# Projecting V eight key tiles at a time and only in some steps of a two-layer cross attention

## What is computed

```python
def _lora_linear(x, W, A, B):
    return x @ W + SCALING * (x @ A @ B)
# layer 0
q = _lora_linear(hidden_states, Wq, Aq, Bq); k, v = the same of the context with 8 heads
attn = softmax(q k^T / 4); out = hidden_states + _lora_linear(attn v, Wo, Ao, Bo)
# layer 1, on the output of layer 0, the same context
Q, K, V = x @ Wq.T + bq, ctx @ Wk.T + bk, ctx @ Wv.T + bv
scores = where(mask, Q K^T / 4, -inf)
y = x + softmax(scores) V @ Wo.T + bo
return (y - mean(y)) / sqrt(var(y) + 1e-5) * ln_g + ln_b
```

## Time and profile before

| | |
|---|---|
| Time, median of 3 runs | 1937.78 us (1935.24 to 1938.48) |
| The profiled execution: its time, and its span | 1935.51 us, 1933.7 us |
| TensorE busy | 1825.2 us, 94% of the span |
| VectorE busy | 1268.2 us, 66% |
| ScalarE busy | 1027.6 us, 53% |
| GpSimd busy | 186.0 us, 10% |
| TensorE clock granted | 0.973 of full speed on average |

### The profile page before, as it was taken

The page is one execution under the profiler, slowest core; times in us unless marked ns, Lnnn a source line. Parts: engine busy times, 40 slices in busy tenths (PEclk is TensorE's granted clock), DMA queues, the critical chain, the costliest instruction groups (busy, mean ns, idle before and its releaser), DMA issues.

```text
span 1933.7 us, 43919 instructions
## 1 busy us (share of the span) xinstructions
PE 1825.2 (94%) x18340; PEld 1134.5 (59%) x18340; DVE 1268.2 (66%) x2743; ACT 1027.6 (53%) x2040; POOL 186.0 (10%) x268
## 2 busy tenths in 40 slices
PE   6899999999999999999999999999999999999985
PEld 3556455565454655555566666666667566666652
DVE  1566666666677777766665667767676767767751
ACT  0055555555555555555554555655555555655562
POOL 2010111102120001021100100001000100001001
PEclk8799999999999999999999999999999999999996
DMA  6911325212352222225422544233533236324300
GB/s 189 243 46 27 78 61 156 52 23 65 78 149 37 42 44 61 42 77 145 84 48 47 107 75 88 41 54 50 110 54 54 38 54 121 48 34 64 50 6 11
DMA packets 65030, 138.13 MB, mean 71 GB/s; under 512 B 12540, under 2 KB 49436, under 8 KB 64832
## 3 DMA queue, kind: packets, MB, share of 16 engines
q1 hardware_dynamic: 64832, 135.33, 34.5%
HBM read 97.84 MB, written 34.89 MB: 69 GB/s over the span
## 4 chain that ended last, share of the span: by engine, by line
PE 84%; ACT 6%; DVE 5%; issue 2%; DMA 2%; SPq 1%; POOL 1%; POOLq 0%
PE value L733 21%; PE work L644 12%; PE score L710 11%; PE work L627 11%; PE score L715 10%; PE ring L690 7%; ACT p_sb L799 4%; PE work L666 3%; PE work L764 3%; DVE chunk_max L904 3%; PE ring L678 2%; PE ring L743 1%; PE work L650 1%; DMA ctx_sb<-ctxT 1%; DMA k_stack<-k_dram 1%
## 5 line engine op out<-in xcount | busy, mean ns | idle before, releaser
L799 ACT ACTIVATE p_sb<-score 124x512 f32<-124x512 f32 (+1 forms) x1664 | 905.3, 597 | 746.6 <-PE score L710 391.0
L904 DVE TENSOR_REDUCE chunk_max<-ring 128x1 f32<-128x402 f32 x2048 | 1071.3, 571 | 318.1 <-PE ring L690 296.2
L690 PE MATMUL ring<-k_stack,q_stack 64*128 64x402 f32 x2048 | 766.3, 433 | 18.9 <-DVE chunk_max L904 13.5
L733 PE MATMUL value<-p_sb,v_sb 124*32 124x256 f32 x6656 | 447.4, 390 | 0.0
L690 PEld LDWEIGHTS ring<-k_stack,q_stack 64*128 64x128 f32 x2048 | 349.1, 186 | 64.9 <-DVE chunk_max L904 52.2
L715 PE MATMUL score<-q_stack,k_stack 64*124 64x256 f32 (+1 forms) x1664 | 332.2, 316 | 19.0 <-ACT p_sb L799 16.4
L710 PE MATMUL score<-q_stack,k_stack 64*124 64x512 f32 (+1 forms) x832 | 331.0, 466 | 9.9 <-ACT p_sb L799 7.9
L644 PE MATMUL work<-wv,ctx_sb 64*124 64x128 f32 x3840 | 323.2, 281 | 9.4 <-ACT v_sb L828 1.7
L644 PEld LDWEIGHTS work<-wv,ctx_sb 64*124 64x124 f32 x3840 | 284.0, 185 | 37.9 <-PE work L644 17.8
L715 PEld LDWEIGHTS score<-q_stack,k_stack 64*124 64x124 f32 (+1 forms) x1664 | 219.3, 184 | 138.7 <-ACT p_sb L799 71.6
L627 PE MATMUL work<-ctx_sb,wk 64*128 64x402 f32 x1280 | 284.9, 515 | 15.7 <-DMA ctx_sb<-ctxT 9.3
(11 more groups left out here) (68 smaller groups left out, 598.8 us busy)
## 6 DMA issues: line engine op xcount, KB each, us to landing
k_stack<-k_dram SPq DMA_DIRECT2D x288, 200.1 KB
k_dram<-k_parts SPq DMA_DIRECT2D x60, 402.0 KB, 3.0
ctx_sb<-ctxT SPq DMA_DIRECT2D x24, 992.0 KB, 6.2
k_dram<-k_parts SPq DMA_DIRECT2D x20, 395.0 KB, 2.6
q_stack<-few_rows SPq DMA_DIRECT2D x256, 2.0 KB
wq<-l_Wq SPq DMA_DIRECT2D x2, 1024.0 KB, 10.0
xt_sb<-xT SPq DMA_DIRECT2D x4, 512.0 KB, 12.3
wo<-l_Wo SPq DMA_DIRECT2D x2, 1024.0 KB, 7.0
```

The costliest lines, as they stand in the source:

```text
L690: engine.matmul(ring[bank_of["max", n]][:, 0:MW], q_stack[rows, u % 3, j, q * P:(q + 1) * P], k_stack[rows, 2 * (z % 3) + (u % 2 if u < L0 ...
L733: done = engine.matmul(value_bank[32 * j:32 * j + 32, 0:S], v_sb[0:tn, seq % 2, i, head * VW:head * VW + 32], p_sb[0:tn, (2 * n + j % 2) % ...
L799: engine.activation(p_sb[0:tn, n % PLACES, :], score_bank[n % 2][0:tn, :], ACT.Exp, scale=SCALE).then_inc(s_exp, 1)
L904: engine.tensor_reduce(chunk_max[:, u % 2, half, j * QT + q, c:c + 1], ring[bank_of["max", n]][:, 0:MW], AX.X, ALU.max).then_inc(s_taken[" ...
```

## The change

V of a sequence becomes two products in place of seven (`groups`): the first has eight tiles, four in each bank of `work` with 128 columns each, and 32 pieces; the second has tiles 8 to 11, two in each bank, and the last tile behind them in the second bank, 20 pieces. There is one swap of the halves in each, and the last tile waits for the pieces before it. ScalarE reads each bank with one instruction (the last tile with one more), without a scale by validity; the added column of ones keeps it, and masked keys have the score -1e30 added. The first product spans two chunks of the context and frees both together.

The rate of the background is multiplied by 13/7 in free steps and is zero in value steps. Budget that is left over can still be spent there. A finished product is read at once in the order of steps. In the prologue there is no V product ahead of the first max.

```diff
+        self.groups = []
+        for first in range(0, NT, 2 * CT):
+            n = min(2 * CT, NT - first) // 2
+            single = first + 2 * n if first + 2 * n == NT - 1 and NT - first < 2 * CT else None
+            self.groups.append((first, n, single))
...
-        values = [("v", 0, g) for g in range(-(-self.NT // 2))]
-        self.product(*values[0])
-        self.product(*values[1])
-        ahead = [(name, p) for name in values[2:] for p in range(self.pieces(name))]
+        ahead = [(("v", 0, g), p) for g in range(len(self.groups)) for p in range(self.pieces(("v", 0, g)))]
...
-    COST = {"k": 670, "v": 213, "q": 213, "o": 853}
+    COST = {"k": 670, "v": 218, "q": 218, "o": 853}
...
                 self.current, self.stopped = None, True
+                self.flush()
...
+        free = [i for i in range(NT) if (i - 1) % NT not in self.ends]
...
-                rate, self.stopped = self.plan_rate(), False
+                rate, self.stopped = self.plan_rate() * (NT / len(free) if i in free else 0), False
...
-        def halves(p):
-
-            swap = p // KT
-            return ((swap, HALF[0], p % KT), (1 - swap, HALF[1], p % KT))
+        def halves(p, tiles=1):
+
+            swap, j, k = p // (KT * tiles), p // KT % tiles, p % KT
+            return ((swap, HALF[0], j, k), (1 - swap, HALF[1], j, k))
...
+                    first, tiles, single = plan.groups[g]
+                    if p < 2 * KT * tiles:
+                        swapped(e, ("v", seq, g), p, tiles)
+                        for n, rows, j, k in halves(p, tiles):
+                            t0 = tile(first + n * tiles + j)[0]
+                            done = engine.matmul(work[0:TT, n, j * P:(j + 1) * P], ctx_sb[rows, k, t0:t0 + TT],
+                                                 w[rows, k, col * P:(col + 1) * P], start=(p == 0),
+                                                 stop=(p == 2 * KT * tiles - 1 and (n == 0 or single is None)))
...
+                        if k == 0 and tiles:
+                            e.wait_ge(s_made["v"], made["v", seq, g] - 1)
...
-                    if seq >= B:
-                        b = (seq - B) // 4
-                        e.wait_ge(s_taken["turn mask"], 1)
-                        engine.activation(dst, src, ACT.Copy, scale=valid[0:tn, b, i:i + 1])\
-                            .then_inc(s_taken["v"], 1)
+                    engine.activation(
+                        v_sb[0:tn, seq % 2, i:i + count, 0:8 * VW].rearrange("p i (h e) -> p i h e", e=VW)[:, :, :, 0:HD],
+                        work[0:tn, bank, block * P:(block + count) * P].rearrange("p (i h d) -> p i h d", i=count, d=HD),
+                        ACT.Copy).then_inc(s_taken["v"], 1)
```

More of the change, by code:

```diff
@@ L51, in step, with tiles_of, readings @@
         self.steps.append(name)
-    def banks_of(self, name):
-        return 1 if name[0] == "v" and 2 * name[2] + 1 == self.NT else 2
+    def tiles_of(self, name):
+        return self.groups[name[2]] if name[0] == "v" else (0, 1, None)
+    def readings(self, g):
+        first, n, single = self.groups[g]
+        return ([(0, 0, first, n), (1, 0, first + n, n)] if n else []) + \
+            ([(1, n, single, 1)] if single is not None else [])
     def begin(self, name, banks):
@@ L63, in begin @@
             self.work_owner[n] = name
-        self.count[name[0]] = self.count.get(name[0], 0) + len(banks)
+        ends = len(banks)
+        if name[0] == "v":
+            _, n, single = self.tiles_of(name)
+            ends = 2 * (n > 0) + (single is not None)
+        self.count[name[0]] = self.count.get(name[0], 0) + ends
         self.made[name] = self.count[name[0]]
@@ L77, in read @@
         elif kind == "v":
-            for n in range(self.banks_of(name)):
-                self.step("read v", name[1], 2 * name[2] + n)
+            for n in range(len(self.readings(name[2]))):
+                self.step("read v", name[1], name[2], n)
         elif kind == "q":
@@ L115, in piece @@
                 self.step("ones", name[1])
[L116 to L120, removed]
+            self.begin(name, [0, 1])
+            self.taken[name] = self.made[name] // 2 if name[0] == "q" else self.made[name]
+            if self.tiles_of(name)[1]:
                 self.swap_count += 2
@@ L158, in ctx_of @@
         if kind == "v":
-            return z, [2 * g // self.CT]
+            first, n, single = self.groups[g]
+            return z, sorted({i // self.CT for i in range(first, first + 2 * n + (single is not None))})
         return z, sorted({c for k in (2 * g, 2 * g + 1) for c in self.chunks_of_keys[k]})
     def names_of_ctx(self, z):
-        B, k, v = self.B, range(self.NM // 2), range(-(-self.NT // 2))
+        B, k, v = self.B, range(self.NM // 2), range(len(self.groups))
         if z < B:
@@ L248, in main_products @@
         B, UB, NT, L0, UNITS = self.B, self.UB, self.NT, self.L0, self.UNITS
-        k, v = range(self.NM // 2), range(-(-NT // 2))
+        k, v = range(self.NM // 2), range(len(self.groups))
         todo = self.todo
@@ L624, in tensor @@
                     swapped(e, ("k", seq, g), p)
-                    for n, rows, k in halves(p):
+                    for n, rows, _, k in halves(p):
                         lo = keys_of(2 * g + n)[0]
@@ L635, in tensor @@
                     if p == 0:
-                        z, (c,) = plan.ctx_of(("v", seq, g))
+                        z, chunks = plan.ctx_of(("v", seq, g))
                         bank_free(e, ("v", seq, g))
-                        e.wait_ge(s_ctx[c], 16 * (z + 1))
+                        for c in chunks:
+                            e.wait_ge(s_ctx[c], 16 * (z + 1))
                         weight_ready(e, "v", layer)
[L640 to L647, removed]
-                    else:
-                        t0, tn = tile(2 * g)
-                        done = engine.matmul(work[0:tn, 0, 0:P], ctx_sb[:, p, t0:t0 + tn],
-                                             w[:, p, col * P:(col + 1) * P], start=(p == 0), stop=(p == KT - 1))
-                        if p == KT - 1:
@@ new lines, in tensor @@
+                    first, tiles, single = plan.groups[g]
[6 more added lines that the diff above has]
+                                                 stop=(p == 2 * KT * tiles - 1 and (n == 0 or single is None)))
+                            piece_done(done, "v", p, tiles)
+                    else:
+                        (t0, tn), k = tile(single), p % KT
+                        if k == 0 and tiles:
+                            e.wait_ge(s_made["v"], made["v", seq, g] - 1)
+                        done = engine.matmul(work[0:tn, 1, tiles * P:(tiles + 1) * P], ctx_sb[:, k, t0:t0 + tn],
+                                             w[:, k, col * P:(col + 1) * P], start=(k == 0 and not tiles),
+                                             stop=(k == KT - 1))
+                        if k == KT - 1:
```

29 lines of the change are left out of this document (13 added, 16 removed).

## The result

The changed kernel takes 1943.54 us (median of 20 runs, 1936.52 to 1949.6), the kernel before 1936.05 us in the same measurement (20 runs, 1931.55 to 1942.73). The ratio is 1.0033, with a 95% interval from 1.002 to 1.0046. It is slower by 0.33%, where I forecast 1907 us. The profiled execution's span is 1941.9 us.

What follows compares the result with a forecast made beforehand. TensorE was taken as the bound, except in free steps, set by a score bank's round. Layer 1 -23, layer 0 -9, prologue +5 and V reads -1 gave 1935.5 - 28 = 1907.5, said as 1907 us; range 1872 to 1948.

Steps and rivals of the forecast that it cites:

- Layer 0: Layer 0's units: zero for dense units 3 to 15, -0.5 us each for 16 to 27, -3 for 28 to 35; -9 together.
- The prices of the pieces: TensorE's projection work: 0.214 us for each piece of V, 0.67 us for each K piece.
- The pair's sum: Units 46 and 47 of layer 1: all steps, work, swaps and starts together 52.1 us against 53.4, -1.3 us.
- The starts of V's products: TensorE waiting for ScalarE's reads of both banks when a V product starts: 1.1 us, twice for a pair of units.
- rival (a): Product starts come a step later and their stalls vanish: 36 us less, 1872 us; chance 0.17.
- Layer 1's size: All 26 units counted in layer 1: -0.9 us for each, -23 us, since other units swap more often.
- The prologue: Start of the kernel, V's first two products moved into the loop behind: +5 us, 2 of it for the clock.
- TensorE go cold: Skill rule against the change: without V products over the prologue's wait, the loop starts at half speed, +8 instead of +5.
- The shadow of the fourth max: Value steps with four maxima: hidden places for pieces given up, about 1.3 us a unit; layer 1 still gains at most 0.6.
- Rival (b): Hidden places ahead of the fourth max decide: 81 us of them given up, some 1955 us, slower; chance 0.17.
- The grouping and the free steps: Layer 1: three fewer swaps, 1.05 us a pair; pieces moved into free steps gain at most 0.6 us a unit.

Runs made afterwards that it cites:

- undoing the order in two ways: Changed kernel with finished products read at the end of their step, 1925.03 us; changed kernel with the maxima's transpose and transfer ahead of the projections, 1925.75 us.
- the line alone: The kernel before with one line added, so that a finished product is read at once: 1940.55 us, ratio 1.0032.
- the run with the loads at the end: Changed kernel with product reads and context loads at the end of the step, loads behind the maxima's transfer: 1915.1 us, 0.991 to the kernel before.

## Why the prediction was wrong

**The step that failed** is one that the prediction doesn't have. "A finished product is read at once" stands in the account of the change, and no term of the sum prices it. I followed the read on ScalarE, where it stands behind the scores' exponentials anyway, and didn't follow it past SyncE's queue: the read of a K product issues two writes of K on that queue, which wait for GpSimd (an instruction of 0.9 to 1.0 us after one of 0.5 for each), and behind them, in order, stands the transfer of maxima on which the next unit's first score waits. The same holds for the context's loads, of which three now come in the same step. Shown: undoing the order in two ways gave 16 and 14 us, undoing it for the loads as well gave 24, and the line alone made the kernel before slower by 0.32%.

**Layer 0 without those waits** gained 8.3 us in units 0 to 27 (773.94 to 765.65), 6 were forecast. Units 28 to 35 gained 4.6 in the changed kernel's profile and 1.5 in that of the run with the loads at the end (forecast 3). The prices of the pieces held: 0.214 us forecast, 0.22 measured.

**The pair's sum** came out at 51.92 us against 52.1 (free steps 23.20 and value steps 28.72 us, where its terms make 23.3 and 28.8), but in part by luck. The starts of V's products were priced at 1.1 us, two in a pair, 44 us over 20 sequences. The changed kernel's trace has 6.9 us of TensorE's waits for ScalarE ahead of V's matmuls, in 13 places, and 4.3 us ahead of Q's. Against that stand pieces left in a value step (four in step 4 of unit 47), which the sum had in free steps. So what rival (a) names was there in part, without its 36 us.

**Layer 1's size was wrong.** I carried the pair 46 and 47 (forecast -1.3, measured -1.5 us) to all of layer 1 as -0.9 for each unit. Units 36 to 59 gained 5.8 us, not 22. The twelve units of the pair's kind gained 8.3 us together, 0.7 each; the twelve in whose stretch an output product and a layer norm fall lost 2.5. Nearly all that is missing lies in three of these: units 41, 49 and 57 lost 11.3 us together, and the other 21 of the 24 gained 17.1. In these three VectorE's sums stand ahead of a step with four maxima; moving them gave 4.7 us back there in one pair of profiles and 4.8 in another. The sum had no term for it. What the rest of their loss comes from is open.

**The prologue** was forecast at +5 and cost 0.6 in these profiles. The nine other profiles with the new prologue have the first score at 97.89 to 99.14 us, those of the three others with the old one at 95.75 to 97.25, so 1 to 2 us is nearer. TensorE did wait for the first max up to 61.69 us, as said, 0.8 us less than in the kernel before (62.45). The timeline of TensorE behind it:

```profile
61.69 0.70 PE L713 MATMUL ring<-k_stack,q_stack 64*128 64x402 f32 x2 [9.95 <-issue]
...
63.72 0.71 PE L713 MATMUL ring<-k_stack,q_stack 64*128 64x402 f32 x2
...
65.76 0.71 PE L713 MATMUL ring<-k_stack,q_stack 64*128 64x402 f32 x2
...
67.24 0.44 PE L713 MATMUL ring<-k_stack,q_stack 64*128 64x402 f32 x2
...
68.31 0.48 PE L713 MATMUL ring<-k_stack,q_stack 64*128 64x402 f32 x2
...
74.24 1.14 PE L664 MATMUL work<-wv,ctx_sb 64*124 64x128 f32 x16 [1.03 <-ACT v_sb L844]
```

The turns of the loop take 2.03, 2.04 and 1.48 us and then 1.1 to 1.2, not the 1.24 that I took; two maxima take 1.14. The kernel before had lost time in its own loop, where VectorE was busy for 10.17 of 14.15 us, since swaps and starts of five products stood there. The windows of that loop and of the first two turns in the changed kernel (the columns as above, the granted clock third from the end):

```profile
62.45:76.60 14.15, 12.11 (x157) 9.92 (x158) 10.17 (x20) 2.06 (x9) 0.00 (x0) 1.00 1.05 383
```

```profile
61.69:66.00 4.31, 4.31 (x38) 4.31 (x40) 2.12 (x4) 0.00 (x0) 0.00 (x0) 0.50 1.05 387
```

The slow turns follow 9.95 us in which TensorE stood idle, and cost 0.9 + 0.9 + 0.4 = 2.2 us against turns of 1.1. The clock is at 0.50 in them, its lower level, and at 1.00 in the whole loop of the kernel before. The Trainium skill, "TensorE: Matmul & The Clock Gate", section "Loop structure matters more than you think", has TensorE go cold, to half its clock, over such a wait, and this trace agrees. I had weighed that against the change with 5 us for the loop, and taken 2. The start of the second V product waited 1.03 us for ScalarE (the row at 74.24), where 1.1 was forecast.

**The shadow of the fourth max** was in the forecast as a loss that the others outweigh. That was right in sign: the new wait for VectorE is 32 us. Used together with full free steps it gave 44 us, 0.7 us for each of 62 units. Rival (b) names this mechanism, but it is not why the change lost: with the order mended the kernel gains 17 us without it.

**The grouping and the free steps** were priced as two parts that add up. They don't: alone the groups give -12 us and the free steps +34 us, both together, with reads and loads at the end, -17 us.

**Two sums of the prediction don't come out.** 1907.5 and the 2.3 us of the median make 1909.8, not 1907. Rival (b)'s own terms, +31 - 11.5 + 5 on 1935.5, make 1960, not 1955. Neither touches the account above.

## What to carry to other kernels

A step that moves in a hand-written order moves every instruction that it issues on every engine: go through the list engine by engine, the transfer queue first, and ask what stands behind each one that waits. A place in which nothing is computed may still be a place in which work is hidden: look for the wait in front of the last instruction of a kind (here the fourth max) before all work is taken away from it. And an average over units is a forecast only for units of the same kind; take one window of each kind.

## What the runs showed that I had not expected

SyncE's queue, which issues in order, turned 3.7 us of delay in issue (315.54 to 319.25) into 8.6 us of idle TensorE: the score that needs the maxima could start only at 329.36. Their transfers came behind about 3 MB issued from 315.09 on (two loads of 992 KB and one of 226, two writes of K of 0.4 MB each), of which about 1 MB had moved by then (an estimate: 4.16 us at the 229 GB/s of that stretch). At unit 4 the same delay in issue (200.83 to 204.58), behind the two writes of K alone, cost 1.8 us of idle TensorE. With only the context's loads ahead unit 8 started 4.3 us late, with nothing ahead under 0.9. So the bytes that stand in the queue ahead of a small transfer count beside the time at which it is issued; no run separates the two at unit 8.
